# Scan layer of a macaron network on one NeuronCore: softplus and the first tap of the convolution on ScalarE, a reordered front, and 24 unread products on TensorE

## What is computed

```python
x_b, res = jnp.split(x @ in_proj_w.T + in_proj_b, [D_INNER], axis=-1)      # D_INNER 256
xc = conv(x_b)                   # causal, per channel, 4 taps, + conv_b
x_b = jax.nn.silu(xc)
x_dbl = x_b @ x_proj_w.T
delta, b, c = jnp.split(x_dbl, [DT_RANK, DT_RANK + D_STATE], axis=-1)      # 8, 16, 16
delta = jax.nn.softplus(delta @ dt_proj_w.T + dt_proj_b)
a = -jnp.exp(A_log)
# per channel d and state n:  h = exp(delta*a) * h + delta*b*u ;  y = sum_n h * c
y = _selective_scan(x_b, delta, a, b, c)
y = (y + x_b * D_param) * jax.nn.silu(res)
return y @ out_proj_w.T + out_proj_b
```

## Time and profile before

| quantity | value |
|---|---|
| median of three runs | 599.19 us (597.4 to 600.1) |
| the profiled execution, device time | 593.37 us |
| its span | 591.6 us |
| busy share of the span: PE, DVE, ACT, POOL | 83%, 79%, 47%, 54% |
| first to last scan start (L947) | 318.9 to 535.3 us |
| mean granted clock of PE | 0.924 of full speed |

### The profile page before, as it was taken

The page is one execution under the profiler, slowest core; times in us unless marked ns, Lnnn a source line. Parts: engine busy times, 40 slices in busy tenths (PEclk is TensorE's granted clock), DMA queues, the critical chain, the costliest instruction groups (busy, mean ns, idle before and its releaser), DMA issues.

```text
span 591.6 us, 10116 instructions
## 1 busy us (share of the span) xinstructions
PE 493.6 (83%) x3866; PEld 297.1 (50%) x3866; DVE 464.7 (79%) x902; ACT 276.1 (47%) x423; POOL 320.1 (54%) x232
## 2 busy tenths in 40 slices
PE   4997989999999999997894887686778768788995
PEld 2774677677777687665321232232223223235674
DVE  4579678587578457766977899999989998998752
ACT  1333665655555334644687472354235324330652
POOL 3147211203000102475104888999999999998573
PEclk9998999999889699998976799889879887999998
DMA  7000000000000000000056632344444333300011
GB/s 205 2 0 2 3 2 2 2 3 4 1 2 4 1 0 2 1 1 1 0 197 254 276 143 99 138 190 162 192 164 191 143 142 142 142 0 2 2 32 40
DMA packets 12322, 42.74 MB, mean 72 GB/s; under 512 B 2857, under 2 KB 8754, under 8 KB 10226
## 3 DMA queue, kind: packets, MB, share of 16 engines
q1 hardware_dynamic: 11458, 41.56, 18.4%
q10 hardware_dynamic: 816, 0.53, 0.3%
HBM read 40.78 MB, written 1.31 MB: 71 GB/s over the span
## 4 chain that ended last, share of the span: by engine, by line
PE 43%; DVE 17%; issue 17%; POOL 16%; ACT 7%; DMA 1%; POOLq 0%; DVEq 0%; ACTq 0%
POOL hC L1025 7%; PE bk L445 6%; PE bk L456 5%; PE bk L661 5%; PE bk L647 5%; DVE hst L947 5%; PE bk L1108 3%; PE bk L636 3%; POOL dBu L1008 3%; DVE xnT L279 2%; PE bk L624 2%; PE bk L1038 2%; ACT g L760 2%; POOL powers L293 2%; PE bk L616 2%
## 5 line engine op out<-in xcount | busy, mean ns | idle before, releaser
L1025 POOL TENSOR_TENSOR hC<-hst,rows 128x1024 f32<-128x1024 f32 x63 | 153.5, 2455 | 12.9 <-DVE hst L947 12.9
L1108 PE MATMUL bk<-hC,ident 128*128 128x512 f32 x256 | 135.3, 664 | 19.4 <-POOL hC L1025 13.5
L947 DVE TENSOR_TENSOR_SCAN hst<-bk,dBu 128x1024 f32<-128x1024 f32 x64 | 144.7, 2276 | 3.0 <-POOL dBu L1008 1.8
L1221 ACT ACTIVATE bk<-delta,aneg 128x1024 f32<-128x1024 f32 x64 | 71.5, 1118 | 114.8 <-DVE hst L947 114.2
L286 POOL TENSOR_TENSOR veps<-mv,lneps 128x4 f32<-128x4 f32 x24 | 5.0, 209 | 164.7 <-DVE mv L258 164.6
L1108 PEld LDWEIGHTS bk<-hC,ident 128*128 128x128 f32 x256 | 51.1, 208 | 80.3 <-issue 51.9
L496 ACT ACTIVATE rows<-bk 128x512 f32<-128x512 f32 x64 | 38.2, 597 | 71.5 <-PE bk L445 71.5
L534 DVE TENSOR_REDUCE smax<-bk 128x4 f32<-128x512 f32 x64 | 43.7, 683 | 27.4 <-PE bk L636 27.4
L927 DVE TENSOR_TENSOR dBu<-bk,du 128x1024 f32<-128x1024 f32 x48 | 57.8, 1204 | 8.4 <-PE bk L1088 8.3
L760 ACT COPY g<-bk 128x512 f32<-128x512 f32 x64 | 37.4, 584 | 49.5 <-PE bk L647 49.0
L1088 PE MATMUL bk<-s,sel 96*128 96x512 bf16 x96 | 31.8, 415 | 32.2 <-DVE dBu L927 29.3
(11 more groups left out here) (176 smaller groups left out, 795.0 us busy)
## 6 DMA issues: line engine op xcount, KB each, us to landing
rows<-c_rows SPq DMA_DIRECT2D x16, 2048.0 KB, 7.1
rows<-c_rows SPq DMA_DIRECT2D x4, 1024.0 KB, 9.5
x<-in_x_dram SPq DMA_DIRECT2D x4, 256.0 KB, 4.9
out_dram<-x SPq DMA_DIRECT2D x4, 256.0 KB, 2.3
wmoe<-in_w_dram ACTq DMA_DIRECT2D x2, 256.0 KB, 4.2
wup<-in_upT_dram SPq DMA_DIRECT2D x1, 256.0 KB
wdn<-in_downT_dram SPq DMA_DIRECT2D x1, 256.0 KB
wproj<-in_in_wT_dram SPq DMA_DIRECT2D x1, 256.0 KB
```

Of the source, the lines that this page charges most:

```text
L947: nc.vector.tensor_tensor_scan(hst[k % 3][:, :], dA[k % 2][:, :], dBu[k % 3][:, :], 0.0, ALU.mult, ALU.add).then_inc(m2["scan"], 1)
L1025: nc.gpsimd.tensor_tensor(hC[k % 4][:, :], hst[k % 3][:, :], crep[:, k % 12, :], ALU.mult).then_inc(m2["hC"], 1)
L1108: last = nc.tensor.matmul(bk01[:, r * CH:(r + 1) * CH], ident[:, :], hC[k % 4][:, r * CH:(r + 1) * CH], start=(k % NS == 0), stop=(k % NS ...
L1221: nc.scalar.activation(dA[k % 2][:, :], delta[:, i, :], ACT.Exp, scale=aneg[:, h * NS + n:h * NS + n + 1]).then_inc(m2["dA"], 1)
```

## The change

DVE's three softplus instructions per unit and four of ACT's go; ACT does softplus with one instruction per unit, units 0 and 1 in the front and units 2 and 3 together after the decay of step 12, each pair between two loads of a function table. Tap 0 of the convolution moves from DVE to ACT, right behind take_conv_in. ACT's front is put in another order, as is PE's; PE gets 6, 6 and 12 bf16 products of 128x512 whose results nobody reads. PE's spread_B(0) waits for the softplus of two units, where it waited for the copy of z of unit 1. x_proj(1, 1) stands one step earlier, and add_state(3) and add_state(7) one step later.

```diff
@@ ssm1_vector
             def conv(c, r):
-                link = stepper(dve, m1["cstep"], c * (DC - 1))
-                dve.wait_ge(m1["xb"], (c + 1) * HV)
-                if c >= 2:
-                    dve.wait_ge(m1["u"], c - 1)
+                link = stepper(dve, m1["cstep"], c * (DC - 2))
+                dve.wait_ge(m1["tap"], c + 1)
                 acc = cacc[c % 2]
-                for k in range(DC):
+                for k in range(1, DC):
                     for h in range(HV):
-                        src = xb[:, r, h, k:k + CH]
-                        if k == 0:
-                            last = nc.vector.tensor_scalar(acc[:, h, :], src, cw[:, h, k:k + 1], cb[:, h:h + 1],
-                                                           ALU.mult, ALU.add)
-                        else:
-                            last = nc.vector.scalar_tensor_tensor(out=acc[:, h, :], in0=src, scalar=cw[:, h, k:k + 1],
-                                                                  in1=acc[:, h, :], op0=ALU.mult, op1=ALU.add)
+                        last = nc.vector.scalar_tensor_tensor(out=acc[:, h, :], in0=xb[:, r, h, k:k + CH],
+                                                              scalar=cw[:, h, k:k + 1], in1=acc[:, h, :],
+                                                              op0=ALU.mult, op1=ALU.add)
...
+        def take_tap(act, c):
+            act.wait_ge(m1["xb"], (c + 1) * HV)
+            if c >= 2:
+                act.wait_ge(m1["u"], c - 1)
+            for h in range(HV):
+                last = nc.scalar.activation(cacc[c % 2][:, h, :], xb[:, c % CPB, h, 0:CH], ACT.Identity,
+                                            scale=cw[:, h, 0:1], bias=cb[:, h:h + 1])
+            last.then_inc(m1["tap"], 1)
@@ ssm1_scalar
             for c in range(NC):
                 take_conv_in(act, c)
+                take_tap(act, c)
@@ ssm2_vector (the functions soft_t, soft_s, soft_delta go)
-            soft_t(0)
-            soft_s(0)
-            soft_delta(0)
             dve.wait_ge(m2["delta"], 1)
...
-                if i + 1 < len(UNITS):
-                    if n == 9:
-                        soft_t(i + 1)
-                    if n == 10:
-                        soft_s(i + 1)
-                    if n == 11:
-                        soft_delta(i + 1)
@@ ssm2_tensor
+            def idle(to, n):
+                for _ in range(n):
+                    nc.tensor.matmul(to, sel[:, 0, :], sel[:, 0:4, :].rearrange("p n q -> p (n q)"),
+                                     start=True, stop=True)
+
             for r in range(CPB):
                 x_proj(0, r)
+            pe.wait_ge(m1["xT"], NC)
+            idle(bank5, 6)
             dt_proj(0)
             take_off(0, 4 * NS, m2["hi"])
+            pe.wait_ge(m1["xb"], NC * HV)
+            idle(bank[1], 6)
             dt_proj(1)
+            take_off(0, 2 * NS, m2["mid"])
             x_proj(1, 0)
-            take_off(0, 2 * NS, m2["mid"])
+            idle(bank[1], 12)
...
                 if k == 0:
-                    pe.wait_ge(m2["zc"], 1)
+                    pe.wait_ge(m2["delta"], HV)
                 elif k == 8 or k == 12:
-                    pe.wait_ge(m2["zc"], k // 4)
+                    pe.wait_ge(m2["zc"], k // 4 - 1)
...
-                if k == 2:
+                if k == 1:
                     x_proj(1, 1)
...
-                if k == LAG + 1:
-                    add_state(0)
+                if k in (LAG + 1, 8, 12):
+                    add_state(k - 1 - LAG)
                 if k == 7:
                     dt_proj(2)
-                if k == 11:
+                elif k == 11:
                     dt_proj(3)
-                if k > LAG:
+                elif k > LAG:
                     add_state(k - LAG)
@@ ssm2_scalar (soft_abs, soft_exp, soft_w, soft_ln go)
+            def softplus(i):
+                if i < HV:
+                    act.wait_ge(m2["dt"], i + 1)
+                    z = z_of[i]
                 else:
+                    act.wait_ge(m2["zc"], i - 1)
+                    z = delta[:, i, :]
+                nc.scalar.activation(delta[:, i, :], z[:, :], ACT.Softplus).then_inc(m2["delta"], 1)
...
             take_u(act, NC - 2)
-            nc.scalar.preload_act_table_set(table)
             take_mid(0)
-            soft_abs(0)
-            soft_exp(0)
-            soft_w(0)
             take_lo(0)
-            soft_ln(0)
-            take_z(1)
-            nc.scalar.preload_act_table(ACT.Silu)
             take_u(act, NC - 1)
-            nc.scalar.preload_act_table_set(table)
+            nc.scalar.preload_act_table(ACT.Softplus)
+            softplus(0)
+            softplus(1)
+            nc.scalar.preload_act_table(ACT.Exp)
             decay(0)
...
-                if i + 1 < len(UNITS):
-                    if n == 6:
-                        soft_abs(i + 1)
-                    if n == 7:
-                        soft_exp(i + 1)
-                    if n == 8:
-                        soft_w(i + 1)
-                    if n == 9:
-                        soft_ln(i + 1)
+                if k == 12:
+                    nc.scalar.preload_act_table(ACT.Softplus)
+                    softplus(2)
+                    softplus(3)
+                    nc.scalar.preload_act_table(ACT.Exp)
```

More of the change, by code:

```diff
@@ L216, in macaron_kernel @@
         m1 = {k: sem("m1_" + k) for k in (
-            "xT", "proj", "xb", "cstep", "conv", "u", "g")} | layer_norm_semaphores("m1")
+            "xT", "proj", "xb", "tap", "cstep", "conv", "u", "g")} | layer_norm_semaphores("m1")
         m2 = {k: sem("m2_" + k) for k in (
-            "xp", "xdbc", "hi", "rest", "mid", "s3", "dt", "abs", "e", "w", "ln",
-            "t", "s", "delta", "zc", "du0", "du", "B", "dBu", "dBup", "dA", "scan", "hC", "sum", "y", "yg", "op", "xupd", "bias", "hClast")}
+            "xp", "xdbc", "hi", "rest", "mid", "s3", "dt", "delta", "zc", "du0", "du", "B", "dBu", "dBup", "dA", "scan", "hC", "sum", "y", "yg", "op", "xupd", "bias", "hClast")}
         c_out = [sem(f"c_out{b}") for b in range(B)]
@@ L1152, in ssm2_scalar @@
         def ssm2_scalar(act):
-            table = "natural_log_exp_and_others"
             def take_xdbc(b):
@@ L1173, in take_z @@
                 nc.scalar.copy(delta[:, i, :], z_of[i][:, :]).then_inc(m2["zc"], 1)
-            def soft_abs(i):
-                e, w, ln, t, z = soft_buffers(i)
-                if i == 0:
-                    act.wait_ge(m2["dt"], 1)
-                else:
-                    act.wait_ge(m2["zc"], i)
-                    act.wait_ge(m2["delta"], i)
-                    act.wait_ge(m1["proj"], NC * PROJ)
-                nc.scalar.activation(e[:, :], z[:, :], ACT.Abs).then_inc(m2["abs"], 1)
-            def soft_exp(i):
-                e, w, ln, t, z = soft_buffers(i)
-                act.wait_ge(m2["abs"], i + 1)
-                nc.scalar.activation(e[:, :], e[:, :], ACT.Exp, scale=-1.0).then_inc(m2["e"], 1)
-            def soft_w(i):
-                e, w, ln, t, z = soft_buffers(i)
-                act.wait_ge(m2["e"], i + 1)
-                if i == 1:
-                    act.wait_ge(m2["dt"], HV)
-                    act.wait_ge(c_out[0], 16)
-                if i == 2:
-                    act.wait_ge(m2["dt"], len(UNITS))
-                    act.wait_ge(c_out[1], 16)
-                nc.scalar.activation(w[:, :], e[:, :], ACT.Identity, bias=1.0).then_inc(m2["w"], 1)
-            def soft_ln(i):
-                e, w, ln, t, z = soft_buffers(i)
-                nc.scalar.activation(ln[:, :], e[:, :], ACT.Ln, bias=1.0).then_inc(m2["ln"], 1)
+            def softplus(i):
+                if i < HV:
+                    act.wait_ge(m2["dt"], i + 1)
+                    z = z_of[i]
+                else:
+                    act.wait_ge(m2["zc"], i - 1)
+                    z = delta[:, i, :]
+                nc.scalar.activation(delta[:, i, :], z[:, :], ACT.Softplus).then_inc(m2["delta"], 1)
             def take_sum(i):
@@ L1209, in take_sum @@
                 else:
-                    act.wait_ge(m2["delta"], 2)
+                    act.wait_ge(m2["dt"], HV)
+                    act.wait_ge(c_out[0], 16)
                 nc.scalar.copy(ysb[:, :], bk01[:, :]).then_inc(m2["y"], 1)
@@ L1218, in decay @@
                     act.wait_ge(m2["scan"], k - 1)
-                elif k == 0:
-                    act.wait_ge(m2["s"], 1)
                 nc.scalar.activation(dA[k % 2][:, :], delta[:, i, :], ACT.Exp,
```

20 lines of the change are left out of this document (removed).

## The result

| | before | changed |
|---|---|---|
| median of 20 runs each | 596.69 us (591.07 to 602.13) | 588.08 us (583.59 to 591.63) |
| ratio, 95% interval | | 0.9861 [0.9836, 0.9887] |
| profiled execution | 593.37 us | 588.01 us |
| its span, PE's mean clock | 591.6 us, 0.924 | 586.3 us, 0.918 |

A forecast was written before the change was run, and what follows sets the result against it. No single engine bounds the whole program (PE 43% of the chain); in the scan POOL and DVE are nearly full. Scan 16.9 plus front 2.4 make 19.3 us, off 599.19: 579.9 us, own range 576.5 to 583, with rivals 574 to 587.

The forecast's parts named there:

- Softplus in the scan: Scan: without softplus on DVE, POOL's 86 instructions take 2.370 us each, 203.8 us, 16.9 less than 220.7.
- a rival at 0.13: Scan: POOL runs without any gap, so the scan gives 22.5 us and the kernel takes 574.3; chance 0.13.
- the table rival: ACT's four table switches each cost some 1.4 us more than the load; gain near 13.7, 585.5 us; chance 0.03.
- the first window: POOL's first 19 instructions in the scan: from 2.847 to 2.370 us each, a gain of 9.1 us.
- the excess at the start: Start of scan: the first window's time above 2.370 us per POOL instruction, 9.1 us, taken to go entirely.
- the start of the scan stays slow: First unit of the scan: half of its 9.1 us excess stays, 584.4 us, or all, 589; chance 0.14.
- at PE's lower clock it may cost 1 to 2 us: Scan on PE: moving add_state(3) and add_state(7) one step back, costed at nothing, or 1 to 2 us at lower clock.
- Six of the products lie on this path and cost 1.5. They may pay by the clock: Front on PE: six unread products before dt_proj(1) cost 1.5 us; dt_proj(1) had taken 3.32 after two short waits.
- The lower bound of the front: Front: gain of 0 instead of 2.4 us if PE stays at its lower clock, costing some 3 us more.
- so these cost nothing: Front on PE: the 12 products end at 312.1 us, before the spread of B can start at 312.8, costing nothing.
- the tap: Front: tap 0 takes ACT 1.15 us, x_proj ends 0.4 us late, and the tap's gain is gone.

The follow-up runs named there:

- wide, no products: Changed kernel with dt_proj over 105 rows of x_dbl (added weights zero) and without the 24 unread products: 577.95 us, ratio 0.9714.
- late bias: Changed kernel with POOL's second output bias made to wait for DVE's last product of state and C: 584.15 us, ratio 0.9762.
- wide dt_proj: Changed kernel with dt_proj over 105 rows of x_dbl instead of 9, added weights zero: 578.62 us, ratio 0.9738; same edit on the kernel before: 595.8 us, 0.9977.
- late rows: Changed kernel with SP's first load of C rows, and all behind it, waiting for the last silu of u: 587.3 us, ratio 0.9873.

## Why the prediction was half right

**Softplus in the scan: right.** POOL's second window is 50.8 us long against 56.2 before and 52.1 forecast, the third 51.7 against 55.9 and 52.1, the fourth 54.0 against 54.5. L994 has a mean of 2.347 us (2.35 forecast), and no POOL instruction of over 3 us is left in the scan. In unit 1 POOL runs without a gap, and in units 2 and 3 with one wait each, of 0.89 and 0.88 us, which is close to what I had given to a rival at 0.13. In units 1 and 2 softplus is all that the change touches, so this gain is its own; a kernel with softplus alone was not run. The burst on ACT:

```profile
359.91 1.28 ACT L1209 ACT_TABLE_LOAD   x1
361.21 2.01 ACT L1159 ACTIVATE delta<-delta 128x1024 f32<-128x1024 f32 x2
363.23 1.28 ACT L1212 ACT_TABLE_LOAD   x1
364.52 1.12 ACT L1176 ACTIVATE bk<-delta,aneg 128x1024 f32<-128x1024 f32 x1
```

It takes 4.61 us, where 4.8 was forecast, and a switch is its load: 1.29 to 1.30 from its start to that of the next instruction, here and in the front. So the table rival fell. The Trainium skill's 2.66 us per switch ("ScalarE: Activation LUTs", on the cost of a table load) is not what this trace shows, and the measurement decides. DVE's next wait, at 363.68, is ended by PE and not by a decay.

**First step that failed: the first window, 4.5 of the 11 us.** The scan gave 12.4 instead of 16.9. The three later windows did 2.3 us better than forecast; the first took 51.5 us where 19 x 2.37 = 45.0 stood in the sum, 6.4 too many; the remaining 0.4 lies in where the stretch ends, at DVE's product and not at POOL's bias. The text called it a choice that the excess at the start goes, because x_proj(1, 1) comes a step earlier and the 12 products keep PE busy. It went by 2.6 of 9.1, which is the rival "the start of the scan stays slow", given 0.14. The very wait named there, 2.02 us for the spread of B, stayed (2.05): the clock was up while the products ran and fell again at 326.7, before the add_states of 5.91 us ahead of that spread. Half of the 6.4, 3.2 us, I had looked at and costed at nothing: "at PE's lower clock it may cost 1 to 2 us". The pair of add_states behind dt_proj did run at the lower clock (5.10 and 4.85), and twice. Moving the sums back removes it, holding the clock removes it, and both together remove no more. What stays of the first window (43.0 us at the least to the first `du`, where 17 instructions without a gap would take 17 x 2.305 = 39.2) was not tried.

**Second step: the clock in the front, 4.9 us between forecast and result.** "Six of the products lie on this path and cost 1.5. They may pay by the clock" rests on the wrong account of why dt_proj(1) was slow before. I read the two short waits ahead of it as the cause. They weren't: without a wait the clock falls too (changed kernel), with the wait and 105 rows it holds (wide, no products). The lower bound of the front, "0 if PE stays at its lower clock", named the case but was still too kind, since it left out the two other terms. By stretch: from x_dbl's copy to the third part 10.4 us instead of 7.5, which is 2.9; 0.8 to 1.0 ahead of x_dbl; and 1.0 behind the third part, where the step "so these cost nothing", on the 12 products, failed: they took 3.14 us, as costed, but began at 315.73 instead of 309.1, and the spread stood behind them until 318.70, 1.1 after the second softplus had ended.

**Third step: the tap.** Its pair of instructions takes 1.52 us, not 1.15. I took the silu's row, but the silu has no operand per channel, and the tap has two (weight and bias). The Trainium skill ("ScalarE: Activation LUTs", on the cost of a table load) adds about 93 ns for each pointer operand; two instructions with two each would be 1.15 + 4 x 0.093 = 1.52 by it, an estimate, and this trace agrees. The mechanism was right, x_dbl waits for ACT and not for DVE, but 0.4 us late became 0.8 to 1.0.

**Fourth: DVE's last product.** The forecast had no term for it. In the changed kernel it stands behind two POOL instructions in place of one, in both of its profiles. The Trainium skill ("SBUF — State Buffer", on the two sides of SBUF) describes the port that VectorE and GpSimd share as a lock that the first to start holds for its whole instruction, the other being blocked. The traces agree that one blocks the other: in all 14 the product ends 1.1 us after a POOL instruction does, after the bias where it is long (5.26 here) and after POOL's last product where it is short (3.35 before), and where it is short without the late bias, POOL's bias takes 3.34 or 3.35 instead of 2.34. The bias behind the product keeps it short in all four kernels that have that edit (2.98 to 3.35). That the change brings the long one is not shown: of the ten traces without the late bias seven have it (5.25 to 5.65), among them the kernel before with the wide dt_proj and nothing else.

**Left open.** Which of the two goes first isn't settled. In eight of those ten traces POOL's last product starts 0.45 to 0.49 us ahead of DVE's and POOL's bias 1.82 to 1.86 behind it, and in six the bias goes first (5.25 to 5.28), in two, with the late rows and with the wide dt_proj, DVE's product (2.96, 2.95). So the order of these starts doesn't decide it, what does the traces don't tell, and two profiles of the changed kernel are too few to say that it is always long. Nor do I know why a dt_proj of 9 rows brings the clock down, only that it falls 2.2 to 3.7 us after dt_proj(0) starts in all nine traces that have it, and 9.3 to 13.6 us after it in the five with 105 rows. And what brings the long `wdn` products in the last layer was not tried.

## What to carry to other kernels

A busy PE is not a PE at its full clock: if matmuls with few contraction rows run near a critical stretch, look at the granted clock behind them, and before adding unread products try padding the matmul itself with zero weights, which takes no longer (1.98 us either way). Here the kernel became 1.5% faster by it, of which 7.2 us (1.2%) lie where the padding acts. In the kernel before the same edit won 1.2 us in the front and nothing in the scan up to the first `du` (49.47 against 49.46 us), so cost a faster engine by what it is the bound of. When two engines meet at a shared place, as at DVE's last product, look at that place in every trace before you read a difference of 2 us as the worth of an edit. And when a change has several parts, undo them one by one: in the scan's later units softplus carried the gain, while the products, the tap and the moved sums took some back (with the late bias 1.2% together, by the ratios 0.9887 and 0.9771).

## What the hardware showed unexpectedly

- PE granted 0.51 over 10 us in which it was busy without a gap, with nine-row products of four passes in it (3.78 us); 1.00 with 105 rows (1.88). With 105 rows it holds through dt_proj(1) with a wait of 1.10 us ahead or without; with 9 rows it falls with transfers beside it (share 0.85) or without (0.00).
- Two softplus instructions over 128x1024 take 1.94 us from PSUM and 2.01 from SBUF, no more than two decays (2.15).
- One product on DVE with both operands in SBUF takes from 2.95 to 5.65 us at the same place of the program, by whether POOL's next instruction goes ahead of it; with the same starts to 0.04 us it took 2.95 in one trace and 5.26 in another.
